# Cross-attention with an FP4 feed-forward layer: quantization in halves, short GpSimd instructions, a new prologue and a third score bank

## The reference

```python
x = x + xattn(layernorm(x), ctx, ctx, Wq, bq, Wk, bk, Wv, bv, Wo, bo)   # 16 heads of 16
x = x + ffn(layernorm(x))

def ffn(x):
    gate = fp4_linear(x, w_gate)          # 256 -> 704
    y = fp4_linear(x, w_up)
    return fp4_linear(silu(gate) * y, w_down)

def fp4_linear(x, w):                     # both sides quantized in blocks of 16
    return einsum('bsk,nk->bsn', fp4_quant_dequant(x), fp4_quant_dequant(w))

scale = max(max(abs(block)) / 6, 1e-12)   # per block of 16; then each value over the
                                          # scale goes to the nearest of 0 .5 1 1.5 2 3 4 6
```

## Time and profile before

| | |
|---|---|
| time, median of 3 runs (lowest, highest) | 1791.18 us (1790.6, 1791.48) |
| the profiled execution's own time | 1790.86 us |
| its span | 1789.1 us |
| PE, DVE, ACT, POOL busy | 93%, 80%, 63%, 29% of the span |
| mean granted TensorE clock | 0.978 of full |
| prologue | 80.0 us (up to batch 0's first exponential) |
| batch 0; 1; 2 to 6; 7 | 210.4; 206.5; 207.2 to 208.4; 181.9 us |
| tail | 70.2 us |

### The profile page before, as it was taken

The page is one execution under the profiler, slowest core; times in us unless marked ns, Lnnn a source line. Parts: engine busy times, 40 slices in busy tenths (PEclk is TensorE's granted clock), DMA queues, the critical chain, the costliest instruction groups (busy, mean ns, idle before and its releaser), DMA issues.

```text
span 1789.1 us, 26605 instructions
## 1 busy us (share of the span) xinstructions
PE 1658.9 (93%) x9408; PEld 655.9 (37%) x9408; DVE 1432.7 (80%) x2032; ACT 1133.2 (63%) x2293; POOL 526.3 (29%) x409
## 2 busy tenths in 40 slices
PE   4798889999999999999999999999999999989968
PEld 2332224333433334333443334333443333313325
DVE  6777888878778887879888787788878797788538
ACT  2367567766667667676667666676676766666631
POOL 4316340442107220253204421072202531012203
PEclk8899899999999999999999999999999999999989
DMA  5644432142324313352331423244132422200000
GB/s 147 147 71 110 97 83 44 47 111 57 61 43 108 86 34 55 60 128 48 64 56 51 109 55 61 43 109 89 32 60 54 91 46 53 54 7 10 13 21 12
DMA packets 106224, 117.50 MB, mean 66 GB/s; under 512 B 22884, under 2 KB 87404, under 8 KB 106092
## 3 DMA queue, kind: packets, MB, share of 16 engines
q1 hardware_dynamic: 101408, 111.54, 29.5%
q10 hardware_dynamic: 4684, 4.27, 1.0%
HBM read 76.78 MB, written 30.16 MB: 60 GB/s over the span
## 4 chain that ended last, share of the span: by engine, by line
PE 77%; DVE 12%; ACT 5%; issue 3%; DMA 1%; ACTq 0%; POOL 0%; SPq 0%; DVEq 0%; POOLq 0%
PE pvb L780 20%; PE st L751 20%; PE mx L765 10%; PE misc L687 7%; DVE cmx L1012 5%; PE misc L645 5%; PE misc L652 5%; ACT prob L937 4%; PE misc L699 2%; PE misc L707 2%; PE misc L666 2%; PE misc L695 1%; PE misc L631 1%; PE misc L728 1%; DVE ht L1041 1%
## 5 line engine op out<-in xcount | busy, mean ns | idle before, releaser
L937 ACT ACTIVATE prob<-st 128x512 f32<-128x512 f32 x1630 | 886.5, 598 | 425.2 <-PE st L751 422.6
L1012 DVE TENSOR_REDUCE cmx<-mx 128x2 f32<-128x1024 f32 x768 | 906.1, 1220 | 194.7 <-PE mx L765 191.6
L751 PE MATMUL st<-qstack,kstack 112*128 112x512 bf16 x1630 | 514.1, 387 | 36.2 <-ACT prob L937 23.5
L780 PE MATMUL pvb<-prob,vv 128*32 128x512 f32 (+1 forms) x3328 | 446.7, 609 | 0.6 <-ACT prob L937 0.6
L751 PEld LDWEIGHTS st<-qstack,kstack 112*128 112x128 bf16 x1630 | 130.2, 99 | 527.6 <-issue 255.0
L765 PE MATMUL mx<-kstack,qstack 48*128 48x512 bf16 (+1 forms) x2048 | 254.7, 339 | 26.9 <-DMA qstack<-scr_q 15.8
L1315 POOL TENSOR_TENSOR ht<-ht,rh 128x704 f32<-128x704 f32 x29 | 40.3, 1388 | 420.5 <-DVE rh L988 420.5
L687 PE MATMUL misc<-wguT,rowsT 128*128 128x352 f32 x456 | 153.7, 458 | 0.0
L1279 POOL TENSOR_TENSOR cin<-cin 128x400 f32<-128x400 f32 (+1 forms) x60 | 55.3, 922 | 278.7 <-ACT cin L872 278.7
L765 PEld LDWEIGHTS mx<-kstack,qstack 48*128 48x128 bf16 x2048 | 57.9, 94 | 198.2 <-issue 154.5
L780 PEld LDWEIGHTS pvb<-prob,vv 128*32 128x32 f32 (+1 forms) x3328 | 66.0, 109 | 138.8 <-issue 124.0
(11 more groups left out here) (196 smaller groups left out, 1564.4 us busy)
## 6 DMA issues: line engine op xcount, KB each, us to landing
kstack<-scr_k SPq DMA_DIRECT2D x384, 100.1 KB, 4.4
scr_k<-cin SPq DMA_DIRECT2D x48, 300.0 KB, 3.4
qstack<-scr_q SPq DMA_DIRECT2D x372, 32.0 KB, 1.9
cin<-ctx_in SPq DMA_DIRECT2D x8, 1280.0 KB, 6.6
scr_q<-qp SPq DMA_DIRECT2D x15, 384.0 KB, 5.4
scr_k<-cin SPq DMA_DIRECT2D x16, 300.8 KB, 5.3
xn<-x SPq DMA_DIRECT2D x8, 512.0 KB, 3.9
att<-pvs SPq DMA_DIRECT2D x128, 32.0 KB, 1.9
```

Source lines behind the costliest of these rows:

```text
L751: mm(score_bank(it, n, pair, h)[0:KROWS[kt], :], kstack[:, hd, KOFF[kt]:KOFF[kt] + KROWS[kt]], qstack[:, hd, :], start=True, stop=True).th ...
L780: last = mm(pvb[2 * D * h:2 * D * (h + 1), :], vv[0:w, kt, (HG * g + h) // 2, D * (h % 2):D * (h % 2 + 2)], prob[0:w, n % 2, h, :], start= ...
L937: activate(prob[0:KROWS[kt], n % 2, 2 * pair + h, :], score_bank(it, n, pair, h)[0:KROWS[kt], :], ACT.Exp, scale=SCALE).then_inc(exp_done[ ...
L1012: v.tensor_reduce(cmx[:, g % 2, h0:h0 + 2, at:at + 1], products, op=ALU.max, axis=AX.X).then_inc(max_free, 1)
```

## The change

The change has six parts.
- The quantization of the 1024 columns `xa` is done in two halves of 512 by DVE and POOL in every batch. The rounding numbers of the halves lie in `ht` and not in `mt`. `xround` 0 and 1 stand on POOL ahead of the split of k 2 and of q 1; before, both in one stood behind k 4.
- POOL's additions and multiplications go in pieces of about 256 columns (`short`, `short_scaled`), and its fills by head. The weights' pieces alternate between two tiles for the rounding numbers.
- SLOTS: `o` 1 goes from step 6 to 7 and `xnT` 0 from 7 to 6. DVE_EXTRA: `nm` 3 from step 35 to 36, `values` 3 from 36 to 38, and the quantization's steps.
- The prologue: the context comes in five DMAs, `xnT` goes in the middle of `ctx2`, `q` 0 ahead of the keys, and SP writes the queries out ahead of the keys.
- In batches 0 and 7 a step without jobs may put scores into the bank `misc` too (ScoreBanks); in batch 0 such steps are 19, 22, 23, 26, 29 to 33, 36, 39 to 41, 45 and 46.
- The tail: mean and root once for all rows, and then both halves.

```diff
--- before.py
+++ after.py
+PIECES = [0, 2, 6, 10, NKT - 1]
...
-    6: ([("o", 1, "late")], []),
-    7: ([("xnT", 0, "early")], []),
+    6: ([("xnT", 0, "early")], []),
+    7: ([("o", 1, "late")], []),
...
-    5: ([("ctx2", j, "early") for j in range(7)], []),
-    8: ([("xnT", j, "early") for j in range(2)], []),
+    5: ([("ctx2", j, "early") for j in range(3)] + [("xnT", j, "early") for j in range(2)] + [("ctx2", 3, "early")], []),
+    9: ([("q", 0, "early")], []),
+    10: ([("ctx2", j, "early") for j in range(4, 7)], []),
     11: ([("k", j, "early") for j in range(4)], []),
-    14: ([("q", 0, "early")], []),
...
-    2: [("late", "values", 4)], 3: [("late", "values", 5)], 4: [("late", "values", 6)], 5: [("late", "values", 7), ("late", "stats", 0)], 6: [("late", "stats", 1)],
-    7: [("late", "mean", 0)], 8: [("late", "root", 0)], 9: [("late", "apply", 0)], 10: [("att", "nm", 1)], 11: [("late", "apply", 1)], 12: [("late", "xmax", 0)],
-    13: [("late", "xscale", 0)], 14: [("late", "xmul", 0)], 15: [("late", "xpower", 0)], 17: [("late", "xlast", 0)],
+    2: [("late", "values", 4)], 3: [("late", "values", 5)], 4: [("late", "values", 6)], 5: [("late", "values", 7), ("late", "stats", 0)],
+    7: [("late", "stats", 1), ("late", "mean", 0)], 8: [("late", "root", 0)], 9: [("late", "apply", 0)], 10: [("att", "nm", 1)],
+    11: [("late", "xscale", 0)], 12: [("late", "xpower", 0)], 13: [("late", "apply", 1)], 14: [("late", "xscale", 1)], 15: [("late", "xpower", 1)],
+    16: [("late", "xlast", 0)], 17: [("late", "xlast", 1)],
...
-    29: [("att", "values", 0)], 30: [("att", "values", 1)], 32: [("att", "values", 2)], 33: [("late", "hscale", 2)], 34: [("late", "hpower", 2)], 35: [("att", "nm", 3)], 36: [("att", "values", 3)], 39: [("late", "hscale", 3)], 40: [("late", "hpower", 3)],
+    29: [("att", "values", 0)], 30: [("att", "values", 1)], 32: [("att", "values", 2)], 33: [("late", "hscale", 2)], 34: [("late", "hpower", 2)], 36: [("att", "nm", 3)], 38: [("att", "values", 3)], 39: [("late", "hscale", 3)], 40: [("late", "hpower", 3)],
...
 TAIL_EXTRA = {
-    1: [("late", "values", p) for p in range(4, 8)], 3: [("late", "half", 0)], 4: [("late", "half", 1)], 6: [("late", "hscale", 0)],
+    1: [("late", "values", p) for p in range(4, 8)], 3: [("late", "stats", 0)],
+    4: [("late", "stats", 1), ("late", "mean", 0), ("late", "root", 0)] + [("late", what, k) for k in range(2) for what in ("apply", "xscale", "xpower", "xlast")],
+     6: [("late", "hscale", 0)],
...
-    0: [("late", "bias", 0)], 10: [("early", "k", 0)], 11: [("early", "k", 1)], 12: [("early", "q", 0)], 13: [("early", "k", 2)],
-    14: [("early", "k", 3)], 15: [("early", "k", 4)], 16: [("late", "xround", 0)], 17: [("early", "k", 5), ("early", "q", 1)], 18: [("early", "k", 6)], 19: [("early", "k", 7)],
+    0: [("late", "bias", 0)], 10: [("early", "k", 0)], 11: [("early", "k", 1)], 12: [("early", "q", 0)], 13: [("late", "xround", 0), ("early", "k", 2)],
+    14: [("early", "k", 3)], 15: [("early", "k", 4)], 16: [("late", "xround", 1), ("early", "q", 1)], 17: [("early", "k", 5)], 18: [("early", "k", 6)], 19: [("early", "k", 7)],
...
+class ScoreBanks:
+
+
+
+    def __init__(self):
+        self.bank, self.before, self.last, self.job_after = {}, {}, {}, {}
+        for kind in ("first", "loop", "last"):
+            turn, user, shared = {0: -2, 1: -1}, {}, None
+            for n in range(STEPS):
+                step = [[j for j in side if j[2] in PARTS[kind]] for side in slots(kind, n)]
+                banks = [0, 1] + [2] * (kind != "loop" and not any(step)) + [3, 4] * (kind == "last" and n >= WIDE)
+                for h in range(HG):
+                    b = min(banks, key=lambda c: turn.get(c, -3))
+                    self.bank[kind, n, h], self.before[kind, n, h] = b, shared if b == 2 else user.get(b)
+                    turn[b], user[b] = HG * n + h, (n, h)
+                    if b == 2:
+                        shared = (n, h)
+                    if h % 2:
+                        for job in step[h // 2]:
+                            self.job_after[kind, job], shared = shared, job
+            self.last[kind] = user
+
+
+SCORES = ScoreBanks()
...
+        def rows_rounding(it, k):
+
+            return mt[:, 0:512] if it.kind == "tail" else ht[:, :, :].rearrange("p t n -> p (t n)")[:, 512 * k:512 * (k + 1)]
...
                 sp.wait_ge(c_link, 4)
+                queries_out(it, 0)
                 keys_out(it, 0, range(4))
                 keys_in(it, 0, "early")
 
...
-                    elif what == "xmax":
-                        link(v.tensor_reduce(ax[:, :], blocks(xa[:, :]), op=ALU.max, axis=AX.X, apply_absolute_value=True), part)
                     elif what == "xscale":
-                        link(scaled(sx[:, :], ax[:, :]), part)
-                        link(v.reciprocal(rx[:, :], sx[:, :]), part)
-                        link(below(rx[:, :]), part)
-                    elif what == "xmul":
-                        link(v.tensor_tensor(blocks(xa[:, :]), blocks(xa[:, :]), over(rx[:, :]), ALU.mult), part)
+                        cols = slice(32 * k, 32 * (k + 1))
+                        link(v.tensor_reduce(ax[:, cols], blocks(halves[k]), op=ALU.max, axis=AX.X, apply_absolute_value=True), part)
+                        link(scaled(sx[:, cols], ax[:, cols]), part)
+                        link(v.reciprocal(rx[:, cols], sx[:, cols]), part)
+                        link(below(rx[:, cols]), part)
                     elif what == "xpower":
-                        if "early" in it.parts:
-                            dve.wait_ge(full["q"], it.count("early", 2, 2))
-                        link(v.tensor_scalar(mt[:, :].bitcast(I32), xa[:, :].bitcast(I32), EXPONENT, None, ALU.bitwise_and), part)
-                        v.tensor_scalar(mt[:, :], mt[:, :], 1.0, ROUND, ALU.max, ALU.mult).then_inc(xm_ready, 1)
+                        y, m = halves[k], rows_rounding(it, k)
+                        link(v.tensor_tensor(blocks(y), blocks(y), over(rx[:, 32 * k:32 * (k + 1)]), ALU.mult), part)
+                        link(v.tensor_scalar(m.bitcast(I32), y.bitcast(I32), EXPONENT, None, ALU.bitwise_and), part)
+                        last = v.tensor_scalar(m, m, 1.0, ROUND, ALU.max, ALU.mult)
+                        if it.kind != "tail":
+                            last.then_inc(xm_ready, 1)
+                        else:
+                            link(last, part)
+                            link(v.tensor_tensor(y, y, m, ALU.add), part)
+                            link(v.tensor_tensor(y, y, m, ALU.subtract), part)
...
-                    elif what == "half":
-
-                        two, cols, words = slice(2 * k, 2 * k + 2), slice(32 * k, 32 * (k + 1)), slice(512 * k, 512 * (k + 1))
...
-                g_.memset(kstack[32:64, heads, :].bitcast(F32), 1.0 + 2.0 ** -23 * 0x3F80).then_inc(c_link, 1)
-                g_.memset(qstack[32:64, heads, :].bitcast(F32), 0.0).then_inc(c_link, 1)
+                for hd in range(heads.start, heads.stop):
+                    last = g_.memset(kstack[32:64, hd, :].bitcast(F32), 1.0 + 2.0 ** -23 * 0x3F80)
+                last.then_inc(c_link, 1)
+                for hd in range(heads.start, heads.stop, 2):
+                    last = g_.memset(qstack[32:64, hd:hd + 2, :].bitcast(F32), 0.0)
+                last.then_inc(c_link, 1)
...
+            def short(out, in0, in1, op):
+
+                n = out.shape[1] // 256
+                w = out.shape[1] // n
+                for j in range(n):
+                    cols = slice(j * w, (j + 1) * w)
+                    last = g_.tensor_tensor(out[:, cols], in0[:, cols], in1[:, cols], op)
+                return last
...
                     elif what == "xround":
-                        m = mt[:, :]
-                        pool.wait_ge(xm_ready, c(1, 1))
-                        g_.tensor_tensor(xa[:, :], xa[:, :], m, ALU.add).then_inc(xr_step, 1)
-                        pool.wait_ge(xr_step, c(1, 1))
-                        g_.tensor_tensor(xa[:, :], xa[:, :], m, ALU.subtract).then_inc(xr_ready, 1)
+                        y, m = halves[k], rows_rounding(it, k)
+                        pool.wait_ge(xm_ready, c(2, k + 1))
+                        short(y, y, m, ALU.add).then_inc(xr_step, 1)
+                        pool.wait_ge(xr_step, c(2, k + 1))
+                        short(y, y, m, ALU.subtract).then_inc(xr_ready, 1)
```

More of the change, by code:

```diff
@@ L584, in shared @@
                     kind, j, part = job
-                    prior = BANKS.prior(it.kind, job)
+                    prior, scored = BANKS.prior(it.kind, job), SCORES.job_after.get((it.kind, job))
+                    if scored is not None and len(scored) == 2:
+                        pe.wait_ge(exp_done[scored[1]], it.count("att", STEPS, scored[0] + 1))
                     if prior is not None and prior[0] == "down0":
@@ L723, in context_tile @@
                     _, j, part = job
```

(4 more changed lines are left out.)

157 lines of the change are left out of this document (68 added, 89 removed).

## The result

The changed kernel takes 1805.99 us (median of 4 runs, 1805.02 to 1810.75), the kernel before 1790.93 beside it (1790.6 to 1791.48): ratio 1.0089, 95% interval 1.0071 to 1.0107. It is 15 us slower, where a gain of 21 had been forecast.

What follows compares the result with a forecast made beforehand. PE, 93% busy, was taken as the bound, so gains lay where it waits or runs at half clock. -23.4 - 8.5 + 26.1 - 9.0 - 3.7 - 1.0 - 1.7 = -21.2 gave 1770 us as a median; range 1740 to 1784.

Steps and rivals of the forecast that it cites:

- o 1 and xnT 0: Steps 6 and 7: PE's wait for values 7 goes; -3.79 us in batches 2 to 6, -2.22 in 1 and 7.
- xround 0 ahead of k 2: Step 14 or 15, loop batches: ACT's take of k 4 and PE's scores come 2.7 us later (1.0 to 4).
- k 5 behind xround 1 and q 1: Step 18, loop batches: k 5's split 1.3 us later, half falling into slack, +0.65 a batch (0 to 1.3).
- nm 3 and values 3: Step 37: the gate no longer queues behind them on DVE, -1.22 us in seven batches, -8.5.
- batch 0: Step 23 -4.1 us, steps 32 and 33 -2.5, third score bank -2.4; together -9.0, between -4 and -15.
- prologue: Queries written out ahead of the keys: PE's first product at 38.6 us instead of 42.42, -3.7 (gain 1 to 5).
- batch 7, the rest: Batch 7: beside waits counted elsewhere, the third score bank gives little, -1.0 us.
- tail: First transposes 1.9 us later, half 1 sooner, DVE's stretched instructions shorter; net -1.7, between -4 and +1.5.
- slower: Rival, chance 0.07: xpower 0 one step late (3.7 us) and a whole clock fall, 26 us more, 1796.
- The clock: Loop batches: PE's stall of some 3 us in step 14 costs two thirds of a 1.57 us fall, +1.0 a batch.
- Half 1 comes sooner: Tail: half 1 follows sooner and DVE's stretched instructions there get shorter, within the tail's net -1.7 us.
- Halves on DVE: Eight maxima instructions doubled: +1.3 us of DVE a batch, hidden by PE in loop batches; 8 us if DVE bound.

Runs made afterwards that it cites:

- f2_q_first: Kernel before with o 1 and xnT 0 exchanged, and POOL's split of q 1 put ahead of that of k 5: 1798.15 us, ratio 1.0045.
- e7_old_tail: Changed kernel with POOL's splits of k 2 and k 5 put back first, and the tail's quantization order as before: 1747.25 us, ratio 0.9753.

## Why the prediction was wrong

| Step | forecast | measured |
|---|---|---|
| o 1 and xnT 0 | -23.4 | -23.9 |
| xround 0 ahead of k 2 | 3.7 a batch, +22 | steps 14 and 15, +32.0 |
| k 5 behind xround 1 and q 1 | 0.65 a batch, +4 | steps 18 and 19, +19.8 |
| nm 3 and values 3 | -8.5 | -6.4 in step 37, six batches |
| batch 0 | -9.0 | -4.9, step 40's +3.2 in it |
| prologue | -3.7 | -2.5 |
| batch 7, the rest | -1.0 | -0.6 |
| tail | -1.7 | +2.3 |

- **The step that failed is the price of the two places on POOL's queue: 4.35 us a loop batch, where 8.6 were measured.** That alone is 26 us of the 36 that were missed. The chain of the first wait (DVE's L1165, POOL's rounding, the split of k 2, ACT's take of k 4) was foreseen and is as the trace has it. Its three terms, against the mean of the six batches: 2.7 for the first wait, step 14 grew by 3.5; 0.65 for the second, step 18 grew by 2.0; 1.0 for the clock, steps 15 and 19, where PE is busy at the lower clock, grew by 1.9 and 1.3, together 3.2. So the clock is the largest part of this miss, and the slack in which k 5 was to hide is the next. The remaining 10 us lie mostly in batch 0 (4.1), the tail (4.0) and step 37 (2.1).
- **The rival "slower"** came nearest with 1796, but by luck. Its cause, xpower 0 a whole step late (3.7 us), did not happen: DVE was 0.4 us later than computed. Its 4.3 us more a batch happen to equal the 4.3 that were measured.
- **The first wait.** L1165 ended 1.0 us before step 14 began (761.39 and 762.39), which is 761.7 in the times of the earlier trace rows, and 761.3 had been computed: DVE was 0.4 us later. POOL's four pieces took 2.91 us for 2.5: a piece of 256 columns takes about 0.16 us more than a quarter of 1024. With both, the sum comes to 3.5, which is the mean that step 14 grew by (3.4 to 3.9).
- **The clock.** I counted two thirds of a fall, once a batch, and 1.57 us for each. It fell at both places in all six batches: after waits of 3.30 to 3.58 us at the first and of 2.80 to 3.03 at the second. The five falls in seven that I had counted from were after waits of 1.98. The Trainium skill (TensorE: Matmul & The Clock Gate, Part 1: The HAM clock gate) says that an array left idle falls back to 1.2 GHz; the trace agrees here, with 0.76 over step 15 of batch 3.
- **The second wait.** "Half of it falls into slack" was wrong. There was no slack: ACT had already been waiting 1.74 us for k 5's split, so each us ahead of it counts in full; f2_q_first shows 3.5 to 3.7 us paid for a split of 3.4. Nor was the net 1.3 us: counted from the start of step 18 in batch 3, the rounding in front ended 1.7 us earlier than before and not 2.4 (its four pieces took 2.91 us, not 2.36, and began 0.2 later), the split of q 1 took 3.97 for 3.65, and that of k 5 3.30 for 3.70; together k 5 was ready 1.8 us later, and the step grew by 2.0. And I gave this place no share of the clock. A wait that already exists is the sign that there is nothing left to hide in.
- **values 3.** "There is cover" held in the loop batches. In batch 0 it did not (step 40); there the weights' quantization stands in steps 38 and 40 of DVE's table, which is the likely reason, and no run takes it away. "In seven batches" was one too many: I had read one batch and multiplied, but step 37 of batch 7 took 4.57 us before and after, with nothing to lose.
- **Batch 0.** The stretched instructions did shrink, L1102 (L1063 before) to 0.83 us from 2.46, as computed. The Trainium skill (GPSIMD Engine Reference, Specifications) says that GpSimd shares its SBUF interfaces with VectorE and collides with its instructions of two SBUF inputs; L1102 is one, and the trace agrees. Step 23 fell by 2.2 us, not 4.1, for the step stayed DVE's (6.31 of 6.38 us busy), and its clock was still 0.78. Steps 32 and 33 fell by 1.5, not 2.5. The third bank is open in 17 steps of batch 0, not 16: steps 5 and 7 have no job there either (3.50 and 3.58 us for 3.99), and belong to the list in the section on the change.

```profile
170.25 0.83 DVE L1102 TENSOR_TENSOR nmr<-nmf,nmp 16x128 f32<-16x128 f32 x1
```
```profile
171.42:177.80 6.38, 4.08 (x17) 0.85 (x16) 6.31 (x8) 2.06 (x4) 6.30 (x9) 0.78 0.29 93
205.36:216.24 10.88, 7.52 (x43) 1.85 (x41) 10.71 (x13) 4.13 (x9) 9.80 (x16) 0.84 0.28 39
```

- **The prologue.** The first product came at 38.19 us (38.6 forecast, 42.42 before), but by luck. No run shows the 2.5 us in which the last of the keys' DMAs was to land: the one issued at 34.8 took 6.84 before, and here the last was issued at 36.78 and took 5.67. The product needs only the first six of the twelve, and started when the sixth had landed, at 38.14. Only 2.5 of the 4.2 us were left at batch 0: PE then waited three times for ACT's takes (1.11, 0.59 and 1.13 us), which it had not done before.

```profile
38.19 1.03 PE L809 MATMUL mx<-kstack,qstack 48*128 48x512 bf16 x4 [12.45 <-DMA kstack<-scr_k]
...
46.38 1.61 PE L690 MATMUL st<-ctxT,wk 128*128 128x400 f32 x4 [1.11 <-ACT qp L905]
...
56.81 1.13 PE L697 MATMUL misc<-wv,ctxT 128*128 128x256 f32 x4 [1.13 <-ACT cin L916]
```

- **The tail.** "Half 1 comes sooner" was true and worth nothing: PE has 11 us of gate and up products on half 0 before it needs half 1 (1758.79 to 1770.02). What counts is when half 0 is ready. Counted from the tail's start it came 2.6 us later, not 1.9, and PE waited longer for it (8.62 before); e7_old_tail, with the old order, took just these 2.6 us back:

```profile
1756.93 1.09 PE L716 MATMUL st<-ident,xa 128*128 128x128 f32 x4 [10.48 <-DVE xa L1185]
```

- **Halves on DVE.** A loop batch (batch 3) has 172.7 us of DVE work for 172.0, +0.7, where +1.3 had been counted from rows. An estimate by the figure of the Trainium skill (VectorE: DVE Perf Modes, The TRN2 errata) had been 0.5. Outside steps 6, 7, 14, 15, 18, 19 and 37 no step of a loop batch grew by more than 0.3 us but step 20 of batch 2, so little of it can have been on the path.

## What to carry to other kernels

An engine that works in order and is put to wait for a late producer blocks what stands behind it, so before moving an instruction ahead of others, list who waits for those others and how much they already wait; with a wait there, the whole delay is paid (3.5 to 3.7 us for a split of 3.4 in f2_q_first). Put the work that others wait for first and the work with a late input behind it: the same instructions in another order were 55 us apart. In this kernel the TensorE clock fell after every new wait of about 3 us (twelve of twelve, 0.8 to 2.4 us each), so count such a fall in full, and look at each stage (here the first batch) before multiplying a gain.

## What was not expected of the hardware

- A GpSimd addition of 256 columns takes 0.75 us in the changed kernel, where 1024 took 2.361 and a subtraction of 512 took 1.157 (group of the kernel before, below): from 1024 to 512 the time halves, from 512 to 256 it does not.

```profile
L1279 POOL TENSOR_TENSOR qx<-qx,qp 128x512 f32<-128x512 f32 x16 | 18.5, 1157 | 42.2 <-ACT qp L861 42.2
```

- A step in which PE never waits can be longer than its twin: step 15 took 5.72 us with PE busy 5.68, for 4.35, since the clock fell at the end of the step before and stayed low into it (0.76).
- With the same prologue the time to batch 0's first exponential lay between 76.9 and 80.2 us over nine kernels.
